# A ViT tower kernel with mixture-of-experts steps: the first product and silu one step ahead, the item plan re-spaced

## What is computed

```python
h = tok(x)                                  # (128, 196, 192)
h = h + attn(layernorm(h), proj_w, proj_b)
h = h + ffn(layernorm(h), gate_w, gate_b, w1, w2, w3, sw1, sw2, sw3)
```

## Time and profile before

| | |
|---|---|
| median of 3 runs | 1929.23 us (1926.97 to 1930.57) |
| the profiled execution | 1933.19 us |
| its span in the profile | 1931.4 us |
| busy share of the span: PE, DVE, ACT, POOL | 81%, 58%, 46%, 39% |
| mean granted clock of TensorE | 0.919 |
| input loads (168 of 1792 KB) | 7.5 us from issue to landing |

### The profile page before, as it was taken

The page is one execution under the profiler, slowest core; times in us unless marked ns, Lnnn a source line. Parts: engine busy times, 40 slices in busy tenths (PEclk is TensorE's granted clock), DMA queues, the critical chain, the costliest instruction groups (busy, mean ns, idle before and its releaser), DMA issues.

```text
span 1931.4 us, 29969 instructions
## 1 busy us (share of the span) xinstructions
PE 1563.9 (81%) x9094; PEld 1222.1 (63%) x9094; DVE 1123.9 (58%) x2060; ACT 879.8 (46%) x2809; POOL 759.0 (39%) x761
## 2 busy tenths in 40 slices
PE   2612787998789887988779988898879988898897
PEld 1201664886558765777558765687658765787676
DVE  5847475566647665466646675476657675254521
ACT  2333644556435644536435654356535554234321
POOL 4336234523363234523354242633354233633332
PEclk9855798999889998999989998899999999999999
DMA  9887676667557786676657787667667684223230
GB/s 342 355 325 305 246 262 238 233 261 281 212 211 263 275 284 210 239 268 240 234 197 276 253 283 252 211 253 288 234 212 275 256 291 128 65 61 96 78 98 24
DMA packets 127672, 440.11 MB, mean 228 GB/s; under 512 B 14221, under 2 KB 80930, under 8 KB 105998
## 3 DMA queue, kind: packets, MB, share of 16 engines
q1 hardware_dynamic: 126390, 436.79, 63.4%
q10 hardware_dynamic: 1112, 1.30, 0.3%
HBM read 413.86 MB, written 20.07 MB: 225 GB/s over the span
## 4 chain that ended last, share of the span: by engine, by line
PE 31%; issue 31%; POOL 17%; DVE 9%; DMA 5%; ACT 4%; SPq 1%; POOLq 0%; ACTq 0%; DVEq 0%
PE bank L1491 12%; POOL ffn L752 11%; PE bank L1335 10%; DVE pooled L942 3%; POOL stat L707 3%; DMA xt<-in_x 2%; PE bank L1511 2%; DVE ffn L1248 1%; DMA ffn<-cw_rows 1%; PE bank L1403 1%; ACT xt L797 1%; ACT L905 1%; POOL SPT L686 1%; ACT ffn L905 1%; PE bank L1390 1%
## 5 line engine op out<-in xcount | busy, mean ns | idle before, releaser
L752 POOL TENSOR_TENSOR ffn<-ffn 128x384 f32<-128x384 f32 (+2 forms) x448 | 508.4, 1137 | 1000.7 <-ACT ffn L905 988.3
L1491 PE MATMUL bank<-W2T,ffn 128*128 128x192 f32 (+1 forms) x3600 | 744.6, 346 | 19.9 <-DVE stage L1229 11.4
L1248 DVE TENSOR_TENSOR ffn<-bank,ffn 128x384 f32<-128x384 f32 (+2 forms) x504 | 312.5, 621 | 665.8 <-POOL ffn L752 419.2
L1491 PEld LDWEIGHTS bank<-W2T,ffn 128*128 128x128 f32 (+1 forms) x3600 | 640.3, 201 | 81.3 <-issue 19.5
L905 ACT ACTIVATE ffn<-bank 128x384 f32<-128x384 f32 (+2 forms) x504 | 272.9, 543 | 442.6 <-PE bank L1511 251.9
L942 DVE TENSOR_REDUCE pooled<-xt 128x3 f32<-128x768 f32 (+2 forms) x375 | 448.1, 1196 | 20.5 <-DMA xt<-in_x 19.8
L797 ACT ACTIVATE xt<-xt 128x256 f32<-128x256 f32 x809 | 329.6, 414 | 86.8 <-DMA xt<-in_x 79.2
L1511 PE MATMUL bank<-X2T,Wx 126*128 126x384 bf16 (+2 forms) x720 | 249.2, 363 | 94.8 <-DVE ffn L1248 89.4
L1511 PEld LDWEIGHTS bank<-X2T,Wx 126*128 126x128 bf16 x720 | 69.7, 100 | 162.4 <-DVE ffn L1248 121.5
L1335 PE MATMUL bank<-x0h,WT0h 128*128 128x512 f32 x288 | 143.3, 498 | 23.0 <-DVE ffn L1248 23.0
L797 ACT ACTIVATION_READ_ACCUMULATOR xt<-xt 128x1 f32 x809 | 158.6, 196 | 0.0
...
## 6 DMA issues: line engine op xcount, KB each, us to landing
xt<-in_x SPq DMA_DIRECT2D x168, 1792.0 KB, 7.5
ffn<-cw_rows SPq DMA_DIRECT2D x192, 256.0 KB, 5.5
ffn<-cw_rows SPq DMA_DIRECT2D x192, 192.0 KB, 7.0
out<-stage SPq DMA_DIRECT2D x192, 96.0 KB
...
```

Of the source, the lines that this page charges most:

```text
L752: nc.gpsimd.tensor_tensor(out=cwb[slot][:, 0:n], in0=silu[(g.par + step) % 2][:, 0:n], in1=cwb[slot][:, 0:n], op=ALU.mult).then_inc(scaled, 1)
L1248: v.tensor_tensor(out=h[step % HR][:, 0:n], in0=h_ps(g, step, 1)[:, 0:n], in1=(silu[p] if e == NE else cwb[(c * NE + e) % CW_RING])[:, 0:n ...
L1491: last = mm(o, h[step % HR][:, 128 * t:128 * t + m], W2T[:, e, :], start=(e == 0 and t % 2 == 0), stop=(e == NE), skip_group_check=True)
```

## The change

PE makes the first product of step s+1 in step s, after silu of step s-1 has left its bank; then it waits for DVE's step s-2, makes the second product of step s, and only then runs layer 2 of step s-2. ACT applies silu for step s+1, and POOL multiplies for step s+1, ahead of the items of step s. The last step of a group does this for step 0 of the next. The plan is rewritten: `A_FIRST` is 37 in place of 39; PHT, VHw, VHT, S 0 to 2, exp 0 and sum 0 of the next group stand in steps 45 to 51 of this one; the items after them are moved up, with one or two steps between an item and the one that needs it; the eight `pow` items take 8 columns each, where four took 16. Tiles begin at other steps, `MIX` is {8: 0, 15: 1}, and the gate items run four and six a step. Lines of context are left out.

```diff
@@ -77,67 +77,66 @@
 AQ_PLAN = {
-    0: [("PHT", 0), ("VHw", 0)],
-    1: [("PHT", 1), ("VHT", 0)],
-    2: [("U", 4), ("S", 0)],
-    3: [("U", 5), ("S", 1), ("VHw", 1)],
-    4: [("U", 6), ("S", 2), ("VHT", 1)],
-    5: [("U", 7), ("exp", 0)],
-    6: [("ET", 0), ("sum", 0)],
-    7: [("ET", 1)],
-    8: [("S", 3), ("AH", 0)],
-    9: [("S", 4), ("M", 0)],
-    10: [("S", 5), ("M", 1)],
-    11: [("exp", 1)],
-    12: [("ET", 2), ("sum", 1)],
-    13: [("ET", 3)],
-    14: [("AH", 1)],
-    15: [("M", 2), ("H", 0)],
-    16: [("M", 3), ("H", 1)],
-    17: [("H", 2)],
-    18: [("H", 3)],
-    19: [("stat_q", 0)],
-    20: [("x2", 0), ("H", 4)],
-    21: [("XT", 0), ("H", 5)],
-    22: [("XT", 1), ("H", 6)],
-    23: [("H", 7)],
-    24: [("stat_q", 1)],
-    25: [("x2", 1)],
-    26: [("XT", 2)],
-    27: [("XT", 3)],
-    28: [("GQ", 0), ("GQ", 1)],
-    29: [("G", 0)],
-    36: [("CQ", 0), ("CQ", 1)],
+    0: [("ET", 0), ("U", 4)],
+    1: [("ET", 1), ("U", 5)],
+    2: [("S", 3), ("U", 6)],
+    3: [("S", 4), ("AH", 0), ("U", 7)],
+    4: [("S", 5)],
+    5: [("M", 0)],
+    6: [("exp", 1), ("M", 1)],
+    7: [("sum", 1)],
+    8: [("ET", 2)],
+    9: [("ET", 3)],
+    11: [("AH", 1), ("H", 0)],
+    12: [("H", 1)],
+    13: [("M", 2), ("H", 2)],
+    14: [("M", 3), ("H", 3)],
+    15: [("stat_q", 0)],
+    17: [("x2", 0), ("H", 4)],
+    18: [("H", 5)],
+    19: [("XT", 0), ("H", 6)],
+    20: [("XT", 1), ("H", 7)],
+    21: [("stat_q", 1)],
+    23: [("x2", 1)],
+    24: [("XT", 2)],
+    25: [("XT", 3)],
+    27: [("GQ", 0), ("GQ", 1)],
+    28: [("G", 0)],
+    37: [("CQ", 0), ("CQ", 1)],
 }
-MIX = {11: 0, 17: 1}
-A_FIRST = 39
+MIX = {8: 0, 15: 1}
+A_FIRST = 37
 AK_PLAN = {
-    39: [("fin", 0), ("tok", 0), ("V", 0)],
-    40: [("stats", 0), ("pow", 0)],
-    41: [("pow", 1)],
-    42: [("stats2", 0), ("pow", 2)],
-    43: [("pow", 3)],
-    45: [("Xw", 0)],
-    46: [("Xw", 1)],
-    47: [("Xw", 2)],
-    48: [("Xw", 3)],
-    49: [("X", 0), ("X", 1)],
-    50: [("X", 2), ("X", 3)],
-    51: [("X", 4), ("X", 5), ("Uw", 0)],
-    52: [("keyG", 0), ("keyG", 1), ("GK", 0), ("Uw", 1)],
-    53: [("Uw", 2)],
-    54: [("Uw", 3)],
-    55: [("U", 0)],
-    56: [("U", 1)],
-    57: [("U", 2)],
-    58: [("U", 3)],
+    37: [("fin", 0), ("tok", 0), ("V", 0)],
+    38: [("stats", 0)],
+    39: [("pow", 0)],
+    40: [("pow", 1)],
+    41: [("pow", 2)],
+    42: [("pow", 3)],
+    43: [("stats2", 0)],
+    44: [("pow", 4)],
+    45: [("pow", 5), ("pow", 6), ("PHT", 0), ("VHw", 0)],
+    46: [("pow", 7), ("PHT", 1), ("VHT", 0)],
+    47: [("Xw", 0), ("S", 0), ("VHw", 1)],
+    48: [("Xw", 1), ("S", 1)],
+    49: [("Xw", 2), ("S", 2), ("VHT", 1)],
+    50: [("Xw", 3), ("exp", 0)],
+    51: [("X", 0), ("X", 1), ("X", 2), ("sum", 0)],
+    52: [("X", 3), ("X", 4), ("X", 5), ("Uw", 0)],
+    53: [("keyG", 0), ("keyG", 1), ("GK", 0), ("Uw", 1)],
+    54: [("Uw", 2)],
+    55: [("Uw", 3)],
+    56: [("U", 0)],
+    57: [("U", 1)],
+    58: [("U", 2)],
     59: [("CK", 0), ("CK", 1), ("CK", 2)],
     60: [("CK", 3), ("CK", 4)],
+    61: [("U", 3)],
 }
...
 for _n in range(GATES):
-    AQ_PLAN.setdefault(30 + _n // 5, []).append(("gate_q", _n))
-    AK_PLAN.setdefault(53 + _n // 5, []).append(("gate_k", _n))
+    AQ_PLAN.setdefault(29 + _n // 4, []).append(("gate_q", _n))
+    AK_PLAN.setdefault(54 + _n // 6, []).append(("gate_k", _n))
 ITEMS = [it for plan in (AK_PLAN, AQ_PLAN) for s in sorted(plan) for it in plan[s]]
...
@@ -151,8 +150,8 @@
-LATE = {s: i for i, s in enumerate([40, 44, 46, 48, 50, 52, 53, 55, 57, 59, 61])}
-EARLY = {s: len(LATE) + i for i, s in enumerate([1, 5, 8, 12, 16, 20, 23, 27, 31, 34])}
+LATE = {s: i for i, s in enumerate([38, 42, 45, 47, 49, 50, 52, 54, 56, 58, 60])}
+EARLY = {s: len(LATE) + i for i, s in enumerate([1, 4, 7, 10, 13, 16, 20, 23, 27, 31])}
 assert len(LATE) + len(EARLY) == TILES and max(EARLY) + 2 < A_FIRST
...
@@ -700,9 +699,9 @@
                 if kind == "pow":
-                    a, half = divmod(i, 2)
-                    u = slice(GB * half, GB * half + GB)
-                    if half == 0:
+                    a, part = divmod(i, 4)
+                    u = slice(8 * part, 8 * part + 8)
+                    if part == 0:
                         pool.wait_ge(var_ready, g.at(4, a + 1))
...
@@ -713,7 +712,7 @@
                     works[0] = 0
-                    pool.wait_ge(rstd_ready, g.at(6, 4))
+                    pool.wait_ge(rstd_ready, g.at(10, 8))
                     work(g, nc.gpsimd.tensor_tensor(out=stat[:, 7, :], in0=stat[:, 4, :], in1=stat[:, 5, :], op=ALU.mult))
...
@@ -752,9 +751,12 @@
-            def ffn_pool(g, left):
+            def ffn_pool(g, left, last=False):
                 for step in range(STEPS):
-                    scale(g, step)
+                    if step + 1 < STEPS:
+                        scale(g, step + 1)
+                    elif not last:
+                        scale(g.plus(1), 0)
                     step_pool(g, step, left)
...
@@ -762,13 +764,14 @@
                 step_pool(G(None, -1), step, 2)
+            scale(G(None, 0), 0)
             ffn_pool(G(None, 0), 2)
...
             ffn_pool(G(None, 6), 1)
-            ffn_pool(G(None, 7), 0)
+            ffn_pool(G(None, 7), 0, last=True)
...
@@ -895,14 +898,27 @@
-            def ffn_act(g, left):
+            def silu_act(g, step):
+                c, e = divmod(step, EX)
+                n = CHUNKS[c][2]
+                act.wait_ge(h1_ready, g.at(STEPS, step + 1))
+                back, before = (g, step - 2) if step >= 2 else (g.minus(1), step - 2 + STEPS)
+                if back.k is not None or back.off >= 0:
+                    if before % EX == NE:
+                        act.wait_ge(h_done, back.at(STEPS, before + 1))
+                    else:
+                        act.wait_ge(scaled, back.at(CW_USES, before // EX * NE + before % EX + 1))
+                nc.scalar.activation(silu[(g.par + step) % 2][:, 0:n], h_ps(g, step, 0)[:, 0:n], ACT.Silu)\
+                  .then_inc(silu_done, 1)
+            def ffn_act(g, left, last=False):
                 for step in range(STEPS):
                     c, e = divmod(step, EX)
-                    n = CHUNKS[c][2]
-                    act.wait_ge(h1_ready, g.at(STEPS, step + 1))
-                    wait(act, h_done, g.at(STEPS, step - 1))
-                    p = (g.par + step) % 2
-                    nc.scalar.activation(silu[p][:, 0:n], h_ps(g, step, 0)[:, 0:n], ACT.Silu).then_inc(silu_done, 1)
+                    if step + 1 < STEPS:
+                        silu_act(g, step + 1)
+                    elif not last:
+                        silu_act(g.plus(1), 0)
                     if e == 1 and 0 < c <= QCH:
...
@@ -910,13 +926,14 @@
                 step_act(G(None, -1), step, 2)
+            silu_act(G(None, 0), 0)
             ffn_act(G(None, 0), 2)
...
             ffn_act(G(None, 6), 1)
-            ffn_act(G(None, 7), 0)
+            ffn_act(G(None, 7), 0, last=True)
...
@@ -1066,7 +1083,7 @@
                 elif kind == "stats2":
-                    dve.wait_ge(rstd_ready, g.at(6, 2))
+                    dve.wait_ge(rstd_ready, g.at(10, 4))
...
@@ -1121,7 +1138,7 @@
-                    dve.wait_ge(rstd_ready, g.at(6, 5 + i))
+                    dve.wait_ge(rstd_ready, g.at(10, 9 + i))
                     if i == 1:
...
@@ -1492,24 +1509,34 @@
-            def ffn_pe(g, left, first=False):
+            def layer1(g, step, k):
+                c, e = divmod(step, EX)
+                query, col, n = CHUNKS[c]
+                o = h_ps(g, step, k)
+                w = (k * EX + e) * INTER
+                if query:
+                    w, at = slice(w, w + INTER), slice(col, col + n)
+                    last = products(o[:, 0:n], [WT0h[:, w], WT0l[:, w], WT0h[:, w], WT1s[:, w], WT1s[:, w]],
+                                    [x0h[:, at], x0h[:, at], x0l[:, at], x1h[:, at], x1l[:, at]])
+                else:
+                    last = mm(o[:, 0:n], Wx[:, w:w + INTER], X2T[:, col:col + n], start=True, stop=True)
+                last.then_inc(h1_ready if k == 0 else h3_ready, 1)
+            def ffn_pe(g, left, first=False, last=False):
                 for step in range(STEPS):
-                    c, e = divmod(step, EX)
-                    query, col, n = CHUNKS[c]
+                    if step + 1 < STEPS:
+                        wait(pe, silu_done, g.at(STEPS, step))
+                        layer1(g, step + 1, 0)
+                    elif not last:
+                        wait(pe, silu_done, g.at(STEPS, step))
+                        layer1(g.plus(1), 0, 0)
                     wait(pe, h_done, g.at(STEPS, step - 1))
-                    for k, o in ((0, h_ps(g, step, 0)), (1, h_ps(g, step, 1))):
-                        if k == 1 and step >= 2:
-                            layer2(g, step - 2)
-                        elif k == 1 and not first:
```

(17 more changed lines are left out.)

## The result

The changed kernel takes 1872.07 us (median of 4 runs, 1871.25 to 1874.11) beside 1929.9 for the kernel before: ratio 0.9705, interval 0.9688 to 0.9721. It is 58 us faster, 103 us slower than forecast, and above the range. The span of its profiled execution is 1869.4 us, the mean granted clock 0.927. In its kernel a step's ring is L1523 (the key products), L912 (silu), L751 (POOL's multiply) and L1265 (DVE's).

What follows compares the result with a forecast made beforehand. Ring waits were taken to bound the key steps, PE the query steps. Savings of 140 us (groups one to seven) and 23.6 (last), less 3 (prologue), gave -160.6: 1772.6 profiled, 1769 as median; range 1712 to 1850.

Steps and rivals of the forecast that it cites:

- First product and silu one step ahead: Every expert step: cuts the PE, ACT, POOL, DVE dependency ring, so POOL's input is ready a step early; no separate total.
- The fourth rival: Early first product held by silu's wait heading PE's queue; ring keeps its length, 1865 us, chance 0.02.
- A wait of about 2.2 us in PE's queue ... I count 1.5, in K1: Key steps 9 to 17: H 4 waits for restacked rows, 2.2 us, of which 1.5 counted.
- Coefficients: nothing, if DMA holds: POOL's coefficient rows, wanted a step earlier: 12 us remain against a 7.0 us landing, so no cost.
- Bounds: nothing, or a stage that waits for tiles, 5 us a group. I take 2.5: Tile loads in steps 0 to 17: DMA cost between nothing and 5 us a group, taken as 2.5.
- The rival of half the gain: Data sets the pace of key steps 0 to 26, which stay at 78.8 us: 1835 us, chance 0.20.
- With shorter gaps I take 2.4 GHz: PE's clock in bare steps: full 2.4 GHz; falling as often as before would cost 20 us in all.
- Of such a burst I leave about 1 us: ACT's table load, exponential and reload for silu: of 3.6 us, about 1 us stays uncovered per burst.
- The shared port: DVE operations with two SBUF inputs and POOL's exclude each other: 0.4 us a group more, 3 in all.
- K4 and Q: Key steps 36 to 44 forecast 26.4 us for 36.0, query steps 45 to 62 forecast 79.4 for 74.8.
- Prologue +3: Before the first expert step: 1.5 us more for powers and 1.5 for uncovered tails.
- Last group: The eighth group, without tile sums: 23.6 us shorter, by the same items over key steps 0 to 44.

Runs made afterwards that it cites:

- e1: Kernel before with only the order of the steps changed (first product and silu one step ahead), the old plan kept: 1798.3 us.
- e10: Changed kernel with the H products and what hangs on them one or two steps later, restacking where it was: 1825.7 us.
- e4: Changed kernel with the next group's first coefficient rows asked at steps 60 to 62 in place of 61 and 62: 1844.7 us.
- e12: Old plan in the new step order, with the next group's first coefficient rows asked at steps 60 to 62: 1797.6 us.
- e14: Changed kernel with H later, first coefficient rows asked earlier, and only a quarter of each input tile loaded after the first group: 1755.7 us.
- e11: Changed kernel with H products two steps later and the first coefficient rows asked a step earlier: 1800.8 us.
- e7: Changed kernel with only a quarter of each input tile loaded after the first group: 1761.1 us.
- e6: Changed kernel with every exponential (softmax and gates) replaced by a copy, so no table loads after the first silu: 1834.2 us.
- e18: Changed kernel with only the gates' exponentials replaced by a copy, softmax keeping its own: 1844.0 us.
- e13: Changed kernel with four powers of 16 columns (steps 39, 41, 44, 45) in place of eight of 8: 1870.3 us.
- e2: Kernel before with only the plan changed (items, tiles, gates, eight powers), the old step order kept: 1919.3 us.

## Why the prediction was wrong

Its sign was right, at 0.95, and its likeliest case took 160 us of gain where there were 58.

**First product and silu one step ahead: right, and worth more than its share.** e1 is the step by itself: 129 us. POOL's waits for silu fell from 988 us to 808 in e1 and 877 in the changed kernel. The fourth rival (the head of PE's queue held by silu) is out, though its 1865 is nearest to the measured time: e1 gives 129 us, and PE and its weight loads wait only 25.5 and 30.9 us for silu in the whole program.

**"A wait of about 2.2 us in PE's queue ... I count 1.5, in K1": the first step that failed.** It was 5.4 us for H 0 and 3.7 for H 4 in the fourth group, and I had seen only H 4. I counted steps from the copy, and from there H 0 stays five steps away; from the sending it went from four to three. I took the 8.8 us from copy to landing as fixed. Here it was 15.3: SP began to send 4.2 us after the copy, behind a tile and coefficients, took 4.4 for the four, and 6.7 more passed until they had landed. PE stood, the clock in K1 was 0.77, and K1 grew by 7.1 for a forecast of 2.5 less. e10 gives the price, 46 us, with the shift of the items behind H in it.

**"Coefficients: nothing, if DMA holds": the second.** I counted the five steps of the steady state. At a group's start the first rows are asked in step 61, two steps ahead of use, and the change takes one of these away. Before, POOL waited for them once in the whole program; now 23 times. e4: 27 us. That price is one of the order and the plan together: in e1 the step earlier is taken away too, and there the same edit gains nothing (e12, 1797.6 for 1798.3).

**"Bounds: nothing, or a stage that waits for tiles, 5 us a group. I take 2.5": too small, and at work in the other two as well.** e14 under e11 gives 45/7 = 6.4 us a group, beyond the bound I had set; in the changed kernel it is 111/7 = 15.9 (e7), with the waits for restacked rows down from 66.0 to 12.8 us and those for coefficients from 87.4 to 25.6. The rival of half the gain (data in K0 to K2, 1835) named this mechanism; K0 to K2 measured 86.1, though, over the 78.8 that I had set as its worst, since I let the stages stay as they were and didn't allow that they could grow.

**"With shorter gaps I take 2.4 GHz": wrong in K0 to K2.** There the granted clock was 0.88, 0.77 and 0.89. By the prediction's own sum that is 27 us a group at 1.2 GHz, nearly the 28 of before the change, only in other stages: K3 to Q ran at 1.00. In e7 the fifth group ran at 1.00 throughout. What the clock alone cost, no run took apart.

**"Of such a burst I leave about 1 us": near it on average (1.2, e6), 2.4 in K3** (e18), 1.4 of K3's miss of 4.7. *The shared port* is a part of the rest. DVE's multiply by a table, the gates' L1170 before and L1187 after, in the groups of instructions (busy us, mean ns):
```profile
L1170 DVE TENSOR_TENSOR gt<-gt,before 128x272 f32<-128x272 f32 (+1 forms) x16 | 5.7, 353 | 0.0
```
```profile
L1187 DVE TENSOR_TENSOR gt<-gt,before 128x272 f32<-128x272 f32 (+1 forms) x16 | 23.1, 1443 | 0.5
```
The same sixteen instructions take 17.4 us more. In K3 of the changed kernel POOL multiplies at the time:
```profile
926.65 4.96 POOL L751 TENSOR_TENSOR ffn<-ffn 128x384 f32<-128x384 f32 x5 [4.39 <-ACT ffn L912]
...
928.78 0.98 DVE L1187 TENSOR_TENSOR gt<-gt,before 128x128 f32<-128x128 f32 x1
```
I had estimated 3 us in all for the port, from POOL's share of K3. The operation of 0.98 us at 928.78 lies wholly under POOL's multiplies; in the kernel before none of the sixteen took over 0.44. These two rows agree with the rule of the Trainium skill (SBUF — State Buffer, "Who interferes with whom") that the two kinds of operation exclude each other. After a table burst POOL has a backlog and does five multiplies in a row, and the gate's operations fall under them: without the gate's burst (e18) the same sixteen take 12.8 us and not 23.1. DVE's busy time in K3 was 18.0 us for the 17.1 forecast, 0.9 more; how much of K3's remaining 3.3 us comes from that, no run took apart.

**K4 and Q: right in sum.** Forecast 26.4 + 79.4 = 105.8, measured 104.5. Against e1's 99.6 it is 4.9 more (mean 4.7), near the 4.6 forecast for the moved items. The split was wrong by 3.0 and 1.7, over the edge between them, and the "4.3 us" of power pace was not seen: K4 is shorter than forecast, and e13 has no difference for four or eight.

**"Prologue +3": wrong sign.** DVE's first L1265 comes at 194.9 for 198.6; it is the plan (195.5 in e2, 198.2 in e1). **Last group**: 168.5 for 187.7, 19 us where 23.6 was forecast.

**The error behind the errors**: I costed order and plan as one change, and asked of the plan what its moves win (K3, K4), not what the old plan's wider gaps were hiding. Faster steps make every distance in steps shorter in time, and the new plan cut the distances to H in steps too.
